# SiLU of the conditioned norms as tanh and a multiplication on VectorE, with new slots for the steps

## The reference

```
x = relu(f + dt * (gradients and second differences of f * grids))         # L0
x = layernorm(up(expert(gelu(down(x)))) + x) * g + b                        # L1, exact GELU
out = silu(scale * norm_of_the_whole_sequence(x) + shift)                   # L2, per feature scale, shift
out = out @ W_in + b_in
out = silu(scale * norm_of_the_whole_sequence(out) + shift)
x = out @ W_out + b_out + x
x = ln(x) * (1 + scale3) + shift3                                           # L3
p = softmax(q k^T / 4 + bias, masked)        # 16 heads, a 256 x 256 bias for each head
x = x + (p v) @ Wo + bo
h = ln(x) * g2 + beta2
x = x + (u * sigmoid(1.702 u)) @ W2 + b2,  u = h @ W1 + b1                  # D_FF = 1024
```

## Time and profile before

| | us |
|---|---|
| median of 3 runs | 919.7 (919.68 to 922.29) |
| the profiled execution, its own time | 922.17 |
| its span, first to last instruction | 920.4 |

### The profile page before, as it was taken

How to read it: one execution, slowest core, us unless ns; L and a number is a source line. 1 busy time by engine, 2 the same in 40 slices (tenths; PEclk the granted TensorE clock), 3 DMA queues, 4 the chain that set the end, 5 groups by cost and what they waited for, 6 DMA issues and landing times.

```text
span 920.4 us, 18271 instructions
## 1 busy us (share of the span) xinstructions
PE 858.6 (93%) x5712; PEld 665.7 (72%) x5797; DVE 742.2 (81%) x2372; ACT 729.5 (79%) x1904; POOL 237.2 (26%) x237
## 2 busy tenths in 40 slices
PE   8776978999999999999999999999999999999988
PEld 8564657777777777777777777777777777777767
DVE  8757798888898888888898898898898898876542
ACT  2234879989798879979798888979798888978773
POOL 2232223332222323232132323223123323121000
PEclk9986999999999999999999999999999999999999
DMA  9826463734445463744446462754446363655500
GB/s 253 244 67 183 130 191 100 206 118 118 139 144 158 136 164 95 204 123 138 138 127 173 119 166 90 192 151 135 126 147 175 99 167 108 166 156 143 164 17 24
DMA packets 133098, 130.90 MB, mean 142 GB/s; under 512 B 18281, under 2 KB 123497, under 8 KB 132985
## 3 DMA queue, kind: packets, MB, share of 16 engines
q1 hardware_dynamic: 101616, 112.02, 42.7%
q10 hardware_dynamic: 31386, 17.71, 7.0%
HBM read 112.61 MB, written 17.07 MB: 141 GB/s over the span
## 4 chain that ended last, share of the span: by engine, by line
PE 58%; ACT 19%; DVE 8%; issue 3%; POOL 0%; ACTq 0%; DVEq 0%
PE ff_ps L1427 11%; PE ff_ps L1408 9%; PE PT_ps L1463 8%; ACT Pr L1120 5%; PE G L1191 5%; PE scores_ps L1448 4%; PE G L1183 4%; PE ctx_ps L1485 3%; DVE bias L956 3%; ACT L1120 3%; PE scores_ps L1445 2%; PE ff_ps L1394 2%; ACT ffT L1101 2%; ACT tanh L1097 2%; ACT PT L1133 2%
## 5 line engine op out<-in xcount | busy, mean ns | idle before, releaser
L1120 ACT ACTIVATE Pr<-bias,nmax 128x256 f32<-128x256 f32 x512 | 255.8, 506 | 35.5 <-DVE nmax L956 34.8
L956 DVE CUSTOM_DVE_ANT_0 bias<-scores_ps,bias 128x256 f32<-128x256 f32 x512 | 194.1, 420 | 47.1 <-PE scores_ps L1448 26.7
L1133 ACT ACTIVATE PT<-PT_ps 128x512 f32<-128x512 f32 x256 | 152.4, 596 | 50.8 <-PE PT_ps L1463 46.1
L1463 PE MATMUL PT_ps<-ident,Pr 128*128 128x128 f32 x1024 | 156.0, 274 | 8.1 <-ACT Pr L1120 8.1
L574 POOL TENSOR_TENSOR rstd<-var,half_neg 128x2 f32<-128x2 f32 (+1 forms) x64 | 43.4, 678 | 389.8 <-DVE var L709 244.5
L1463 PEld LDWEIGHTS PT_ps<-ident,Pr 128*128 128x128 f32 x1024 | 119.9, 141 | 16.9 <-ACT Pr L1120 13.3
L1408 PE MATMUL ff_ps<-ctxT,w 128*128 128x256 f32 x480 | 117.2, 387 | 13.0 <-ACT ffT L1101 10.7
L1427 PE MATMUL ff_ps<-w,ffT 128*128 128x256 f32 x480 | 112.9, 381 | 0.0
L1408 PEld LDWEIGHTS ff_ps<-ctxT,w 128*128 128x128 f32 x480 | 86.3, 190 | 33.0 <-ACT ffT L1101 16.2
L1448 PE MATMUL scores_ps<-k_stack,q_stack 96*128 96x256 bf16 x512 | 99.2, 275 | 6.0 <-issue 2.0
L1120 ACT ACTIVATION_READ_ACCUMULATOR Pr<-bias,nmax 128x1 f32 x512 | 100.6, 196 | 0.0
(11 more groups left out here) (232 smaller groups left out, 1615.8 us busy)
## 6 DMA issues: line engine op xcount, KB each, us to landing
bias<-in_fside_Bx16xSxS_dram SPq DMA_DIRECT2D x256, 256.0 KB, 3.2
part_dram<-front ACTq DMA_DIRECT2D x32, 384.0 KB, 2.8
q_stack<-part_dram SPq DMA_DIRECT2D x32, 192.0 KB, 3.8
k_stack<-part_dram SPq DMA_DIRECT2D x32, 192.0 KB, 3.7
F<-in_x_dram SPq DMA_DIRECT2D x16, 256.0 KB, 3.7
ada<-rows_dram SPq DMA_DIRECT2D x16, 256.0 KB, 4.7
q_stack<-part_dram SPq DMA_DIRECT2D x32, 128.0 KB, 3.8
k_stack<-part_dram SPq DMA_DIRECT2D x32, 128.0 KB, 3.5
```

Of the source, the lines that this page charges most:

```text
L956: nc.vector.tensor_tensor_reduce(out=t, in0=SP_[:, n % 2, q * S:(q + 1) * S], in1=t, scale=-1.0, scalar=BIG, op0=ALU.add, op1=ALU.min, acc ...
L1120: ins = nc.scalar.activation(Pr[:, n % PR, q, :], bias[:, n // CH % RING, 2 * (n % CH) + q, :], ACT.Exp, bias=nmax[:, n, q:q + 1], scale=-1.0,
L1133: nc.scalar.activation(PT[:, m % BATCH, :, :].rearrange("p c q -> p (c q)"), TP[:, m % 2, :], ACT.Identity).then_inc(pt_ok, 1)
L1463: ins = pe.transpose(TP[:, m % 2, c * S + q * P:c * S + (q + 1) * P], Pr[:, m % PR, q, c * P:(c + 1) * P], ident[:, :])
```

## The change

Each SiLU becomes three things. ACT runs `Tanh` on the two halves of the norm with halved scale and shift, into `yT`; then ACT runs `Identity` with the same scale and shift on the same halves, in place, which leaves u/2. DVE then multiplies: yT = (yT + 1) * (u/2), one `scalar_tensor_tensor` over 128 x 512 elements. PE's product waits for DVE (`y_ok`), and DVE waits for ACT (`gate_ok`, new). The multiplications have steps of their own, `gate0` and `gate1`. The halving is done once, in `s_condt`, by the second operation of an instruction that was there. Besides, the numbers of `AT` and `AT_LAST` are new almost throughout; `AT_FIRST` has the same numbers as before, with `gate0` and `gate1` added. The tables' rows are cut here to the entries that the text speaks of.

```
-AT = {... "w1": ((25, 26.25, 28, 29.75), (41.75, 42.75, 43, 45.75)), ...
-      "aff0": (12, 28.75), "y0": (12, 28.5), "w_in": (14, 30), "aff1": (18, 34), "y1": (18.5, 33.75), "w_out": (19, 35.75),
-      "q_split": (25.5, 40.25), "k_split": (26.75, 41.75), "v": (28.75, 46), ...}
+AT = {... "w1": ((25.75, 26.25, 28.5, 29.5), (41.5, 43, 43.5, 44.5)), ...
+      "aff0": (12, 28), "y0": (12.5, 28.25), "w_in": (14, 30), "aff1": (17, 33.25), "y1": (17.75, 33.25), "w_out": (19, 36),
+      "q_split": (25.75, 41), "k_split": (26.75, 41.5), "v": (29.25, 43), ...
+      "gate0": (13.75, 29), "gate1": (18.25, 34.75)}
+AT_FIRST = {... as before ..., "gate0": (12.5, 24.5), "gate1": (15.5, 33.25)}
@@ condition columns (s_condt)
-                        nc.vector.tensor_scalar(cond[:, :, m], SP_[:, 0, at:at + B], cb[:, m:m + 1], one,
-                                                ALU.add, ALU.add).then_inc(cond_ok, 1)
+                        halved = m < C_ONESC
+                        nc.vector.tensor_scalar(cond[:, :, m], SP_[:, 0, at:at + B], cb[:, m:m + 1], 0.5 if halved else one,
+                                                ALU.add, ALU.mult if halved else ALU.add).then_inc(cond_ok, 1)
@@ DVE, front
+                    for b in seqs(("gate0", "gate1")[k], j, n):
+                        dve.wait_ge(gate_ok[b], 2 * j + k + 1)
+                        nc.vector.scalar_tensor_tensor(out=yT[b], in0=yT[b], scalar=1.0, in1=(x2T, zT)[k][b],
+                                                       op0=ALU.add, op1=ALU.mult).then_inc(y_ok[b], 1)
@@ ACT, front
-                        for c in range(2):
-                            ins = nc.scalar.activation(yT[b][:, c, :], src[:, c, :], ACT.Silu,
-                                                       bias=cond[:, 2 * j + b, C_SHIFT + c:C_SHIFT + c + 1],
-                                                       scale=cond[:, 2 * j + b, C_SCALE + c:C_SCALE + c + 1])
-                        ins.then_inc(y_ok[b], 1)
+                        for dst, func in ((yT[b], ACT.Tanh), (src, ACT.Identity)):
+                            for c in range(2):
+                                ins = nc.scalar.activation(dst[:, c, :], src[:, c, :], func,
+                                                           bias=cond[:, 2 * j + b, C_SHIFT + c:C_SHIFT + c + 1],
+                                                           scale=cond[:, 2 * j + b, C_SCALE + c:C_SCALE + c + 1])
+                        ins.then_inc(gate_ok[b], 1)
```

More of the change, by code:

```diff
@@ L72 @@
            "masks": 0}
-AT = {"x4": (27.75, 46.25), "ctx_spread": (19.5, 40.5), "ctx": (19.75, 36.25), "ctx_scale": (19.5, 36.25),
[4 rows of a table removed]
-      "out": (35, 51.25), "store": (36.75, 57.5), "prods_p": (0.5, 18.75), "prods": (0.75, 14), "diffs": (2, 16.5),
[8 rows of a table removed]
-      "q_split": (25.5, 40.25), "q_out": (25.25, 42), "k": (25.5, 41), "kf": (25, 40.5), "k_split": (26.75, 41.75),
-      "k_out": (28, 41.75), "v": (28.75, 46), "V": (29, 46.5), "mask": (20, 2)}
-AT_FIRST = {"s_gelu": (3.25, 3.25), "s_sin": (0.25, 0.25), "s_se": (2.75, 2.75), "s_trig": (3.5, 3.5), "s_onehot": (4, 4),
-            "s_grid": (4.25, 4.25), "s_h1": (3, 3), "s_h2": (3.5, 3.5), "s_h2t": (3.75, 3.75), "s_sel": (2, 2),
-            "s_cond": (4.5, 4.5), "s_condt": (6.25, 6.25), "s_mask": (24.25, 24.25), "s_rows": (15.25, 15.25),
-            "x4": (28, 46.75), "s_fill": (4.25, 4.25), "s_bq": (7.75, 7.75), "s_w2": (34.25, 34.25),
-            "prods_p": (0.25, 5.5), "prods": (5.5, 6), "diffs": (5.5, 6.5), "edges": (5.5, 6.5), "l0": (4, 8.75),
-            "x1": (5.75, 12), "relu": (4.25, 7), "x1_turn": (4.75, 16.5), "x1T": (5, 7.25), "res1": (5.75, 13.75),
-            "down": (6.25, 16.75), "hid": (5.75, 7.5), "expert": (6.5, 17.5), "expT": (6.5, 7.75), "up": (8.5, 18),
[7 rows of a table removed]
@@ L103 @@
-AT_LAST = {"ctx_spread": (23.25, 34.5), "ctx": (20.5, 30.75), "ctx_scale": (20.5, 30.75), "wo": (22, 33.75),
[4 rows of a table removed]
-           "w2": ((31.25, 37, 47, 48.25), (67, 73.25, 75.75, 77.5)), "out": (55.25, 70), "store": (57, 68.75)}
+AT = {"x4": (31.75, 49), "ctx_spread": (19.75, 37), "ctx": (20.75, 36.75), "ctx_scale": (20, 36.75),
[4 rows of a table added]
+      "w2": ((31.25, 33.5, 33.75, 35.75), (47.25, 48, 48, 50.25)), "out": (36.5, 50), "store": (36.5, 63),
+      "prods_p": (2, 17.75), "prods": (1, 14.5), "diffs": (2.5, 16.25), "edges": (2.75, 17), "l0": (4, 18.75),
+      "x1": (5, 18.5), "relu": (5.5, 18), "x1_turn": (6.5, 20.25), "x1T": (7.5, 19), "res1": (14.75, 25),
+      "down": (8.25, 21), "hid": (8.25, 20), "expert": (9, 22.25), "expT": (8.75, 21.75), "up": (9.75, 23.25),
[6 rows of a table added]
+      "k_split": (26.75, 41.5), "k_out": (26.5, 42.25), "v": (29.25, 43), "V": (29, 44.5), "mask": (20, 2),
+      "gate0": (13.75, 29), "gate1": (18.25, 34.75)}
@@ new lines @@
+AT_FIRST = {"s_gelu": (3.25, 3.25), "s_sin": (0.25, 0.25), "s_se": (2.75, 2.75), "s_trig": (3.5, 3.5),
+            "s_onehot": (4, 4), "s_grid": (4.25, 4.25), "s_h1": (3, 3), "s_h2": (3.5, 3.5), "s_h2t": (3.75, 3.75),
+            "s_sel": (2, 2), "s_cond": (4.5, 4.5), "s_condt": (6.25, 6.25), "s_mask": (24.25, 24.25),
+            "s_rows": (15.25, 15.25), "x4": (28, 46.75), "s_fill": (4.25, 4.25), "s_bq": (7.75, 7.75),
+            "s_w2": (34.25, 34.25), "prods_p": (0.25, 5.5), "prods": (5.5, 6), "diffs": (5.5, 6.5),
[8 rows of a table added]
+            "q_out": (28, 40.75), "k": (22.5, 40.75), "kf": (28, 40.5), "k_split": (22.25, 41), "k_out": (29, 42.75),
+            "v": (28.5, 43.25), "V": (25.75, 44), "gate0": (12.5, 24.5), "gate1": (15.5, 33.25)}
@@ L109 @@
+AT_LAST = {"ctx_spread": (23.5, 34.75), "ctx": (20.75, 30.75), "ctx_scale": (19, 30.75), "wo": (21, 33.75),
[4 rows of a table added]
+           "w2": ((31.5, 48.5, 49.5, 50), (66.25, 73.75, 76.5, 82)), "out": (66.5, 81.5), "store": (86, 94.75)}
 SP_AT = {"front": (0, 7), "stacks": (1, 2, 9, 11), "mask": 6, "rows": (12, 3)}
@@ L314, in adapter_to_attention_kernel @@
             for n in ("mstat_ok", "mstat_mm", "mstat_read", "affine_ok", "y_ok", "var_ok", "rstd_ok", "stored"))
+        gate_ok = [sem(f"gate_ok{b}") for b in range(2)]
         back_var_ok, back_rstd_ok = sem("back_var_ok"), sem("back_rstd_ok")
```

## The result

The changed kernel takes **937.6 us** in the median (935.6 to 938.9), the kernel before 919.7: a ratio of 1.018 (95% interval 1.016 to 1.020). I had forecast 910 us, range 898 to 925. Both the sign and the range are wrong.

The account below looks back on a forecast made before the run. PE was taken as the bound, busy 858.6 of 920.4 us. Six steady turns -11.4, first turn -1, prologue +3, end 0 gave -9.4 us, so 910 us from the median 919.7; range 898 to 925 (8 in 10).

Parts of the forecast that it names:

- the latency of each SiLU: From ACT to PE's product: some +1.9 us each, less up to 1.28; costed at nothing in steady turns, covered by head work.
- the multiplication by its length: On DVE: 0.86 us each, 32 places +27.5 us, a steady turn +3.4 (+5.4 at 1.35), still under PE's 101.
- Its own fallback: Steady turns: if head work does not cover SiLU's longer latency, a turn costs 4 x 0.6 to 1.9 us.
- The prologue and the first turn: Before the steady turns: +3 us for two lengthened bare SiLU chains, -1 us for the first turn's table loads.
- The table loads: On ACT: 61 fewer, 78.3 us; PE gains 0.47 us a steady turn, its wait behind the one load on the chain.
- The new slots' cover of the W1 waits: On PE in steady turns: the product by wv between W1 pieces covers 1.1 of their 1.39 us of waits.
- 0.3 more: Steady turns: 0.3 us a turn from PE's other waits on ACT, which is 6.3 us freer.
- Rival 3: Steady turns: DVE waits for ACT, blocking its queue and PE's exponentials; slower, 932 us at waits of 3.0 each; 22%.
- rival 2: No change: only the 0.47 us behind the one load is won, 2.8 in six turns, prologue gives it back; 920 us; 15%.
- Rival 1: All comes through: PE's idle time in the steady turns goes, -21.5 us, first turn 3 more; 898 us; 15%.

Follow-up runs that it names:

- e10: Kernel before with the changed kernel's slot tables and one Tanh in place of Silu, no Identity or DVE multiplication (another function's values): 905.8 us, ratio 0.985.
- e3: Changed kernel, but pair 0 alone keeps SiLU on ACT, its conditions not halved and DVE's multiplication left out: 929.1 us, ratio 1.007.
- e7: Changed kernel with the Identity pair left out in pair 0 alone (its SiLU is then wrong): 933.7 us, ratio 1.014.
- e9: Kernel before, old slots, with one Tanh in place of Silu and nothing else (another function's values): 916.9 us, ratio 0.996.
- e2: Kernel before, SiLU on ACT with all its table loads, but with AT and AT_LAST of the changed kernel: 927.2 us, ratio 1.005.
- e12: Changed kernel with the Identity pair left out in all pairs, DVE's multiplication and all slots kept (another function's values): 927.4 us, ratio 1.007.
- e5: Changed kernel with pair 0 keeping SiLU on ACT and step V of b = 1 back behind the gate (slot 46.5): 924.8 us, ratio 1.005.
- e6: e5 with POOL's two gate products issued ahead of the reciprocal deviation of the first affine: 943.4 us, ratio 1.027.
- e8: e5 with the w_in product of b = 0 a quarter slot later (14.25), behind the product of the heads: 934.1 us, ratio 1.015.
- e11: e8 with the last W1 activation behind the copy of the transposes on ACT and its DVE multiplication half a slot later: 954.0 us, ratio 1.037.

## Why the prediction was wrong

**The step that failed** is the one on the latency of each SiLU: "In the steady turns the slots leave at least a slot between multiplication and product in most places ... and head work covers it. I cost it at nothing there". It costs 3.0 us a turn (102.33 in e10 to 105.35), 18.1 us in six, where I had 0. The reading of the slots was wrong, too: of the four places two have a slot or more between multiplication and product (29 to 30, 34.75 to 36), the two of b = 0 have a quarter (13.75 to 14) and three quarters (18.25 to 19). At w_in of b = 0, the one with a quarter, a feed-forward multiplication and V stand ahead of the new one on DVE. I had priced the multiplication by its length (0.86, measured 0.69 in the median, 1.51 at most) and not by where it stands in the queue of an engine that is busy 94 of 105 us. Its own fallback, 4 x 0.6 to 1.9 us a turn without the cover, does hold the measured 3.0, but it stood among no rival and had no chance of its own.

**The prologue and the first turn**, +3 and -1, were the second mistake. Forecast and profile are 24.8 us of span apart (-9.4 and +15.4): 15.6 in the steady turns, 8.9 ahead of them, 0.3 at the end. e10, without second pair and hop, has 1.6 us less than before at the start of pair 1; the changed kernel 10.9 more. By medians, pair 0's SiLU form is worth 8.4 us (e3). I lengthened two of the four bare chains of pair 0, put one at w_out at nothing and left the other out, and priced a microsecond of chain at a microsecond, while three of the four groups of products behind the waits ran slower than before, 3.0 us in all. Nor did I see that w_in of pair 1, b = 0, in the first turn, is as bare: it waits 2.38 us and takes 3.68. e7 shows the part of ACT's second pair in pair 0, 3.8 us.

**What was right.** The table loads: 61 go, ACT 679.7 us. Their own worth, a wait of 0.47 a turn: e9's turn is 0.41 shorter. The new slots' cover of the W1 waits, 1.1 a turn: with the rest, 1.9 us forecast; e10's turn is 2.32 shorter and 102.33 us long, against "steady turns of 102.7 us". Without the prologue's +3 my sum gives 907; e10 took 905.8. So the gain side of the sum was right in size, and the cost side missing. In part that is luck: I had the load wait, the W1 waits and 0.3 more as separate terms, and e2 and e9 show that alone the slots lose 1.0 us a turn and the loads give 0.4.

**The rivals.** Rival 3 had the sign and nearly the time, 932, but not the mechanism: it had DVE blocked by waits for ACT of 2.6 us each. DVE waited for ACT in front of L871 13.3 us in all, 17 times, of which 6.6 us in the six steady turns: 1.1 us a turn, a tenth of the slack that it would have had to use up, and e12 has the loss without these waits. Of rival 2, all that holds is that the prologue takes back more than the loads give. Rival 1, 898 us with turns of 101, is not reached even by e10.

**What stays open.** Whether some order lets this arithmetic beat the kernel before. The three attempts aimed at the 0.73 us at w_in in e5's steady turns and failed; what e5 still loses to the kernel before, in the first turn, none of them addressed. No kernel here that computes the reference beats it (e2 and e5, the nearest, are 0.5% slower). The 905.8 of e10 is another function's time: it says what a SiLU with one activation pair in the exponentials' table would be worth, not that there is one.

## What to carry over

When an operation is split over two engines, price the handover first: list what stands ahead of the new instruction in the second engine's queue, in order, with its durations beside its neighbours on other engines, for every place where it occurs, the bare ones of the prologue above all. Engine time that is freed on an engine off the chain buys little by itself (3 to 4 us for 78), and more once the order is made anew around it (another 11). To learn which part pays, run a cheaper function that has only one part of the new costs (here one Tanh), before the order is tuned for all of them.

## What the runs showed of the hardware

In these rows an operation of DVE on SBUF that meets a POOL multiplication waits it out, and a tiny one pays as much as a large one: the feed-forward multiplication took 1.76 us for 0.69, 1.1 us more. In e5, DVE's L711 on one column, with POOL idle, took

```profile
434.03 0.16 DVE L711 TENSOR_TENSOR nmr<-gs 128x1 f32<-128x1 f32 x1
```

and 1.10 us in e6 beside a POOL multiplication of 1.27, with which it ended (438.89 and 438.88 us). The Trainium skill (SBUF — State Buffer, "SBUF: two separate sides") says that the shared port pair is an exclusive lock and not a split of bandwidth; the trace agrees, down to 128x1.

The same code took 3 us more in the prologue of one execution than in that of another. e3 and e5 are the same program up to the first head, yet its exponentials start at 82.5 us in one and at 85.7 in the other. The stretch where they part, e3 and behind it e5:

```profile
40.00:46.00 6.00, 5.75 (x48) 4.86 (x45) 4.53 (x12) 0.41 (x1) 1.79 (x2) 1.00 1.01 355
```

```profile
40.00:46.00 6.00, 5.75 (x24) 3.96 (x24) 2.54 (x9) 0.00 (x0) 0.25 (x2) 0.50 0.99 346
```

PE is equally busy, but at a granted clock of 1.00 in one and 0.50 in the other, with half the products done. By the other three kernels with this prologue (e6, e8, e11) the first head came at 83.4, 83.2 and 85.7 us. What set the clock differently is not shown. A term for a prologue with idle stretches is not to be read from a single execution; I read pair 0 too high by 2.4 us that way.
